# A top-1 expert layer that sorts its tokens through DRAM and runs each tile of 128 rows through one expert

## The reference

```python
router_logits = x @ Wr.T
expert_idx = jnp.argmax(jax.nn.softmax(router_logits, axis=-1), axis=-1)
inter = jnp.zeros((x.shape[0], W1.shape[2]), dtype=x.dtype)          # [2048, 512]
for e in range(E):
    mask = (expert_idx == e)[:, None].astype(x.dtype)
    inter = inter + mask * jax.nn.gelu(x @ W1[e] + b1[e], approximate=False)
y = inter @ Wo + bo + x
out = (y - mu) * jax.lax.rsqrt(var + LN_EPS) * gamma + beta          # mean and variance of y
...
x = x + 0.5 * _L0_ffn_ref(_layernorm(x, axis=-1), ...)
```

## Time and profile before

| | us |
|---|---|
| median of three runs | 1225.09 (1223.17 to 1226.32) |
| the profiled execution, its own time | 1229.85 |
| its span in the trace | 1227.9 |
| TensorE (matmul) busy | 1100.5 (90%) |
| VectorE busy | 1005.6 (82%) |
| ScalarE busy | 665.1 (54%) |
| GpSimd busy | 65.8 (5%) |
| first matmul of the second expert layer starts at | 604.06 |
| first result of the ternary layer behind it (L982) starts at | 749.19 |

### The profile page before, as it was taken

How to read it: one execution, slowest core, us unless ns; L and a number is a source line. 1 busy time by engine, 2 the same in 40 slices (tenths; PEclk the granted TensorE clock), 3 DMA queues, 4 the chain that set the end, 5 groups by cost and what they waited for, 6 DMA issues and landing times.

```text
span 1227.9 us, 33848 instructions
## 1 busy us (share of the span) xinstructions
PE 1100.5 (90%) x14565; PEld 487.3 (40%) x14565; DVE 1005.6 (82%) x2343; ACT 665.1 (54%) x861; POOL 65.8 (5%) x62
## 2 busy tenths in 40 slices
PE   1998977999999999998699979589999999999978
PEld 1455542333333333333355547333333333333336
DVE  8977569999999998885447557789999999987754
ACT  0322222556777777777332214145667777787753
POOL 5111001000000000000101000100000000000000
PEclk9999988999999999999699999799999999999998
DMA  5100044000000000000000000620000000000001
GB/s 157 36 1 1 1 119 121 5 3 3 2 2 2 3 2 2 3 3 3 1 1 1 1 1 1 181 63 3 2 2 2 3 2 2 2 2 3 3 2 35
DMA packets 23554, 24.05 MB, mean 20 GB/s; under 512 B 3134, under 2 KB 21220, under 8 KB 23404
## 3 DMA queue, kind: packets, MB, share of 16 engines
q1 hardware_dynamic: 22252, 18.73, 5.3%
q0 software_dynamic: 1152, 3.15, 0.9%
HBM read 13.20 MB, written 8.39 MB: 18 GB/s over the span
## 4 chain that ended last, share of the span: by engine, by line
PE 52%; DVE 37%; issue 4%; ACT 4%; DMA 1%; SPq 0%; DVEq 0%; ACTq 0%
DVE part_max L1349 26%; PE psum L1209 11%; PE psum L1231 10%; PE psum L443 10%; PE psum L1183 6%; ACT hidden L1312 3%; PE psum L467 3%; PE psum L1196 2%; PE psum L899 2%; PE psum L914 1%; DVE xn L168 1%; PE psum L1258 1%; PE psum L1237 1%; DVE norm_v L151 1%; PE psum L428 1%
## 5 line engine op out<-in xcount | busy, mean ns | idle before, releaser
L1349 DVE TENSOR_REDUCE part_max<-psum 128x1 f32<-128x512 f32 (+3 forms) x1120 | 676.6, 666 | 59.9 <-PE psum L1237 40.4
L1312 ACT ACTIVATE hidden<-psum 128x1024 f32<-128x1024 f32 (+3 forms) x640 | 538.7, 895 | 231.0 <-PE psum L1196 127.3
L1231 PE MATMUL psum<-k_slots,q_slots 128*32 128x512 f16 (+3 forms) x5120 | 391.0, 355 | 32.9 <-DVE part_max L1349 13.5
L1209 PE MATMUL psum<-hidden,v_aug 128*9 128x512 f32 (+3 forms) x2560 | 291.8, 532 | 0.4 <-ACT hidden L1312 0.4
L1231 PEld LDWEIGHTS psum<-k_slots,q_slots 128*32 128x32 f16 x5120 | 123.5, 95 | 289.2 <-DVE part_max L1349 194.1
L443 PE MATMUL psum<-parts,w_parts 128*128 128x512 f16 x768 | 179.7, 385 | 1.9 <-DVE parts L839 1.9
L1183 PE MATMUL psum<-q_slots,k_slots 32*128 32x512 f16 (+3 forms) x1280 | 146.1, 354 | 18.0 <-ACT hidden L1312 14.0
L443 PEld LDWEIGHTS psum<-parts,w_parts 128*128 128x128 f16 x768 | 73.7, 99 | 82.5 <-issue 5.9
L1183 PEld LDWEIGHTS psum<-q_slots,k_slots 32*128 32x128 f16 x1280 | 43.0, 91 | 146.0 <-ACT hidden L1312 85.1
L587 ACT CAST parts<-psum 128x512 f16<-128x512 f32 x64 | 37.2, 588 | 107.3 <-PE psum L428 107.3
L1237 PE MATMUL psum<-ident_bf,later_keys 128*32 128x128 bf16 (+2 forms) x1408 | 91.8, 251 | 0.0
(11 more groups left out here) (168 smaller groups left out, 721.6 us busy)
## 6 DMA issues: line engine op xcount, KB each, us to landing
q_slots<-q_rows SPq DMA_DIRECT2D x8, 512.0 KB, 3.7
k_slots<-k_rows POOLq DMA_DIRECT2D x24, 128.0 KB, 4.1
q_rows<-parts SPq DMA_DIRECT2D x18, 128.0 KB, 2.9
k_rows<-parts SPq DMA_DIRECT2D x18, 128.0 KB, 2.7
q_slots<-in_L_ffn_W_dram SPq DMA_DIRECT2D x2, 1024.0 KB, 6.8
k_slots<-k_rows SPq DMA_DIRECT2D x8, 128.0 KB, 3.9
q_slots<-nm_parts SPq DMA_DIRECT2D x64, 4.0 KB
out_dram<-x_res SPq DMA_DIRECT2D x4, 256.0 KB, 2.3
```

Source lines behind the costliest of these rows:

```text
L1209: last = pe.matmul(psum[VW * h:VW * h + DH + 1, O_BANK, off:CH], v_aug[:, j, G * g + h, :], probs[:, (2 * n + h // 2) % NP, h % 2, off:CH] ...
L1231: last = pe.matmul(psum[rows32(m), bank, a * w:(a + 1) * w], q_slots[:, g, qb * P + m * SLOT:qb * P + (m + 1) * SLOT], k_slots[:, G * g + ...
L1312: act.activation(probs[:, tile % NP, :, off:CH], psum[:, bank:bank + 2, off:CH], ACT.Exp, scale=scale).then_inc(exp_done, 1)
L1349: dve.tensor_reduce(part_max[:, step_no[s] % 2, h0:h0 + heads, i, kc], psum[:, bank, 0:heads * w].rearrange("p (a k) -> p a k", a=heads), ...
```

## The change

The third layer is now `sorted_expert_layer` (after: L914 to L1287). The first layer is still `expert_layer`.

*Routing.* All four chunks are turned, given logits and `onehot`, and in addition each token's row in a DRAM table is counted out with small matmuls (`ranks`): expert e's region starts at row 2048 e, and a token's row there is how many earlier tokens chose e. GpSimd writes the blocks of `xn` there with 16 indirect DMAs of 128 rows. `tile_table` counts how many tiles of 128 rows each expert needs, gives each of 24 tiles an expert and a start, and puts them into `tile_i`. 24 tiles always suffice, and all 24 are always run.

*Experts.* SyncE waits for all scatters and loads the 24 tiles into `x_sorted`, each with a start read from `tile_i` into a register. Six groups of four tiles then take the place of four chunks of eight masked experts. The expert's weights are picked by a register, so the masks, their copies and products are gone; a group is 4 bias matmuls of 512 columns and 48 of 128 columns.

*Way back.* A finished group is scaled by gamma on GpSimd and stored by SyncE to `sorted_dram`. When all six are stored, GpSimd fetches each token's row by 16 indirect DMAs that add to `x_res`; the next layer normalises a chunk once its four have landed. Of the next layer's chunks one is normalised in this layer (`next_given` = 1) and three in the ternary layer.

*First layer.* 17 short GpSimd instructions set constants, and SyncE writes zeros over the DRAM table, 8 MB in two DMAs. A few semaphores are merged.

```diff
+            @blk.tensor
...
+                def ranks(n):
+                    pe.wait_ge(onehot_ready, n + 1)
...
+                    for i in range(BPC):
+                        out_i = psum[:, RANK_BANK, i * E:(i + 1) * E]
+                        pe.matmul(out_i, ones_bf[:, :], region_rows[:, :], start=True, stop=False)
+                        if n:
+                            pe.matmul(out_i, ones_bf[:, :], before[:, :], start=False, stop=False)
+                        for j in range(i):
+                            pe.matmul(out_i, ones_bf[:, :], onehot[:, n * BPC + j, 0, :], start=False, stop=False)
+                        last = pe.matmul(out_i, earlier[:, :], onehot[:, n * BPC + i, 0, :], start=False, stop=True)
+                    last.then_inc(ranked, 1)
...
+                def experts(n):
...
+                    chosen = [pe.value_load(tile_i[0:1, 0, n * BPC + i:n * BPC + i + 1], min_val=0, max_val=E - 1)
+                              for i in range(BPC)]
+                    pe.wait_ge(lo_ready, n + 1)
+                    for t in range(HT):
+                        if n >= 1:
+                            pe.wait_ge(gelu_done, HT * (n - 1) + t + 1)
+                        pe.matmul(psum[:, t, :], b1_parts[:, t * P:(t + 1) * P],
...
+                        for i in range(BPC):
+                            for wp, xp in ((0, 0), (0, 1), (1, 0)):
+                                weights = w1_parts[:, bass.ds(chosen[i], 1), wp, t * P:(t + 1) * P]
+                                last = pe.matmul(psum[:, t, i * P:(i + 1) * P], weights.rearrange("p a i -> p (a i)"),
+                                                 x_parts[:, n % 2, xp, i * P:(i + 1) * P], start=False,
+                                                 stop=(i, wp) == (BPC - 1, 1))
+                        last.then_inc(experts_done, 1)
...
+                pe.wait_ge(*released)
+                transposes(0)
+                logits(0)
+                for n in range(NCH):
+                    if n + 1 < NCH:
+                        transposes(n + 1)
+                    ranks(n)
+                    if n + 1 < NCH:
+                        logits(n + 1)
+                tile_table()
+                sorted_transposes(0)
+                for n in range(TGROUPS):
+                    experts(n)
+                    if n + 1 < TGROUPS:
+                        sorted_transposes(n + 1)
+                    if n >= 1:
+                        down(n - 1)
+                down(TGROUPS - 1)
...
+            @blk.gpsimd
...
+                for n in range(NCH):
...
+                    pool.wait_ge(placed, n + 1)
+                    for i in range(BPC):
+                        b = n * BPC + i
+                        pool.indirect_dma_start(out=region_dram, out_offset=bass.IndirectOffsetOnAxis(place[:, b:b + 1], 0),
+                                                in_=xn[:, lo + i, :], in_offset=None).then_inc(scattered, 16)
...
+                for n in range(TGROUPS):
+                    pool.wait_ge(group_moved[n], STORED)
+                for c in next_norms.order:
+                    for i in range(BPC):
+                        b = order.index(c) * BPC + i
+                        pool.indirect_dma_start(out=x_res[:, c * BPC + i, :], out_offset=None, in_=sorted_dram,
+                                                in_offset=bass.IndirectOffsetOnAxis(back[:, b:b + 1], 0),
+                                                compute_op=ALU.add).then_inc(arrived[c], 16)
...
+            @blk.vector
...
+                for n in range(NCH):
+                    choose(n)
+                    if given <= n + 1 < NCH:
+                        norms.make(dve, own, s1, order[n + 1])
+                    take_places(n)
+                tile_table()
+                ways_back()
+                low_part(0)
+                for n in range(TGROUPS):
+                    if n + 1 < TGROUPS:
+                        low_part(n + 1)
+                    finish(n)
+                for c in next_norms.order[:next_given]:
+                    next_norms.make(dve, own, s1, c)
...
+            @blk.sync
+            def _(sp):
+                sp.wait_ge(table_ready, 1)
+                sp.wait_ge(scattered, 16 * NB)
+                for k in range(TILES):
+                    start = sp.value_load(tile_i[0:1, 1, k:k + 1], min_val=0, max_val=E * T - P)
+                    sp.dma_start(x_sorted[:, k, :], region_dram[bass.ds(start, P), :]).then_inc(group_moved[k // BPC], 16)
...
-        released = expert_layer(False, orders[2], 2, norms[2], norms[3], released)
-        released = ternary_layer(False, orders[3], 3, norms[3], norms[4], released, projections[4])
+        released = sorted_expert_layer(orders[2], 2, norms[2], norms[3], 1, released)
+        released = ternary_layer(False, orders[3], 1, norms[3], norms[4], released, projections[4])
```

More of the change, by code:

```diff
@@ L31 @@
 NPART = 3
+TILES = 24
+TGROUPS = TILES // BPC
+assert TILES >= NB + E - 1
 TERMS = 3
@@ L179, in __init__ @@
                 self.ready, self.order = sem(name), order
+                self.arrived = None
             def wait(self, engine, chunk):
@@ L184, in make @@
             def make(self, dve, own, scratch, chunk):
+                if self.arrived:
+                    dve.wait_ge(self.arrived[chunk], 16 * BPC)
                 norm_stats(dve, own, scratch, x_res, chunk * BPC, BPC)
@@ L376, in _ @@
                     sp.wait_ge(b1_split_ready, 1)
+                    sp.wait_ge(sorting_set, 2)
                     for r in range(NPART):
@@ L386, in _ @@
                                  k_slots[0:H * MAX_PARTS, 0, :]).then_inc(rest_rows_stored, 16)
-                    sp.wait_ge(rest_rows_stored, 16 * 3)
+                    zeros = k_slots[:, 2:2 + H // 2, :].rearrange("p h t -> p (h t)").bitcast(F32)
+                    for half in range(2):
+                        rows = slice(half * E * T // 2, (half + 1) * E * T // 2)
+                        sp.dma_start(region_dram[rows, :].rearrange("(p r) d -> p (r d)", p=P),
+                                     zeros).then_inc(rest_rows_stored, 16)
+                    sp.wait_ge(rest_rows_stored, 16 * 5)
                     sp.wait_ge(b1_moved, 16 * NPART)
@@ L405, in logits @@
                     if first and n == 0:
-                        pe.wait_ge(wr_ready, 1)
+                        pe.wait_ge(weights_on_dve, 2)
                     for i in range(BPC):
@@ L452, in biases @@
                     for t in range(HT):
-                        pe.matmul(psum[:, t, :], b1_parts[:, t * P:(t + 1) * P], onehot_t[:, n % 2, :],
+                        pe.matmul(psum[:, t, :], b1_parts[0:NPART * E, t * P:(t + 1) * P], onehot_t[:, n % 2, :],
                                   start=False, stop=True).then_inc(experts_done, 1)
@@ L1449, in macaron_layers @@
         orders = (UP, UP, BETWEEN, TURNING, TURNING, DOWN)
-        norms = [Norms(f"xn_ready{i}", order) for i, order in enumerate((UP, UP, BETWEEN, BETWEEN, TURNING, DOWN))]
+        norms = [Norms(f"xn_ready{i}", order) for i, order in enumerate((UP, UP, BETWEEN, TURNING, TURNING, DOWN))]
         projections = {1: Projection(w_qkv0, False, norms[1], orders[1]), 4: Projection(w_qkv1, True, norms[4], orders[4])}
```

323 lines of the change are left out of this document (299 added, 24 removed).

## The result

The changed kernel takes 1270.82 us in the median of four runs (1265.44 to 1273.12) against 1225.70 (1223.17 to 1228.45) of the kernel before on the same chip: a ratio of 1.036 (95% interval 1.032 to 1.040). It is 45 us slower. The forecast was 1286 us in a range of 1258 to 1320. The profiled execution took 1273.08 us.

What follows compares the result with a forecast made beforehand. TensorE was taken to set the pace before; afterwards a serial chain: 51.3+114.5+20.7+19.5 = 206.0 us against 145.1, +60.9, so 1290.8 us profiled and 1286 as a median, range 1258 to 1320.

Steps and rivals of the forecast that it cites:

- A: Routing, from the layer's first matmul until group 0's tiles have landed: 51.3 us.
- B: The six expert groups, from first tile's turning to the last finish: 114.5 us.
- C: Way back: scaling, store, four gathers and landing, normalising, turn, high and low part, all open: 20.7 us.
- D: Ternary layer up to its first result, with three more chunks normalised in the open: 19.5 us.
- the serial turn: Groups 2 to 5: experts, turning, down, finish, low part without overlap, W + 10.4 us; W 7.5 to 10.5, 1277 to 1295, 55%.
- rival 3: Six groups: the group is cheap, W 5.4 to 7, 12 to 22 us less, 1264 to 1274; 17%.
- W: TensorE's expert matmuls of one group: taken as 9 us, bounds 5.4 and 12.4.
- Rival 2: Six groups: slow on TensorE, W = 12.4 gives 1306, a clock staying at 1.2 GHz 1323; 22%.
- The registers' 2 us: Share of each group's expert time on TensorE allowed for register instructions: 2 us.
- Rival 4: Six turns: TensorE's work alone paces, 128-column matmul 0.054, W 3.5, turn 7.7, groups 54, time 1226, not slower; 3%.
- The four landings on the chain: DMA landings of scatter, tile load, store and fetch: 12.8 us from profile rows; 9 by the skill's fit, giving 1282.
- The first layer: Zeroing the DRAM table done near 106 us, before SyncE is next wanted at 154.92: costs nothing.

Runs made afterwards that it cites:

- Experiment 1: Changed kernel with VectorE making the low part of group n+2 ahead of finish(n), not behind it: 1242.91 us, median of four.
- experiment 6: Changed kernel with low parts ahead of finish and tile k fixed to expert k mod 8, no register loads: 1232.36 us, one run.
- experiment 3: Changed kernel with tile k fixed in code to expert k mod 8, no expert registers, output not the reference's: 1271.25 us, one run.
- experiment 7: Experiment 5 plus expert registers loaded inside down(n) and late chunks normalised one choice earlier: 1221.53 us, median of ten, ratio 0.9973 to the kernel before.
- experiment 2: Changed kernel with GpSimd's four beta additions moved behind the last scatter: 1263.36 us, one run.
- experiment 4: Changed kernel with the 16 final indirect fetches writing x_res without adding, output not the reference's: 1262.30 us, one run.
- experiment 5: Changed kernel with low parts ahead, beta additions late, and the ternary layer's fb_half additions on VectorE instead of GpSimd: 1236.41 us, one run.
- experiment 8: Experiment 7 with plain fetches into xn and VectorE adding each chunk to x_res before normalising: 1224.83 us, median of ten, ratio 0.9990 to the kernel before.

## Why the prediction was right, and where its numbers were not

Forecast and measured costs are +60.9 and +44.5 us for the stage. The difference of 16.4 is A -2.8, B -18.8, C +0.3 and D +5.0. That the total is no further off is in part luck: D's error hides 5 us of B's, and A and C are each a sum of errors that cancel.

**The mechanism: right.** The forecast was the serial turn, and everything said of its order is in the trace: `finish` then low part, over 6 us of waiting for L1230, on groups 2 to 5, with the granted clock below 1. Experiment 1 shows it by taking it away. The time is that of rival 3 (1264 to 1274), the same serial turn with a W of 5.4 to 7, which had been given 17%; the forecast's own W of 7.5 to 10.5, with 55%, did not come. The signs read the same way: the wait is there, but turns are 15.5 to 16.7 us apart for 19 to 20, not far above the 15 at which the forecast called itself wrong, L1040 is busy 5.0 us a group for 9, and the last `finish` ends at 748.83 for 770. Rival 2, a clock that stays low, is half there: groups start low and all recover within the group, and down (3.74 us) runs at the full level.

**The mis-sized term: W.** "I take 7 for a group half at the low clock plus 2 for the registers: W = 9." Measured from a group's first bias matmul to the start of what follows it W is 6.39, 4.29, 5.11, 5.85, 6.24 and 6.44, mean 5.7: 19.7 us less over six, which is more than piece B's whole error. B without W is 61.3, forecast 60.5. Two terms failed. The registers' 2 us were the right price in the wrong place: 1.8 a turn where TensorE paces (experiments 1 and 6), nothing behind a wait (3). And 0.095 us for a 128-column pair was read from the length of a group of four (0.38). Such a length contains the whole of one matmul, from start to end: that is 0.219 us, yet 12 take 0.83, which is 0.219 + 11 x 0.0555. The price in a running sequence is 0.0555, a quarter of the 0.216 of 512 columns. Rival 4 had that figure (0.054), and its turn of 7.7 us is the 7.56 of experiments 6 and 7, with the order mended. Its point, "It decides from turns of 7.6 us down", does not hold by the turn alone: in experiment 6 piece B is 59.1 where rival 4 had 54, and the kernel took 1232. Experiment 7 came out 0.3% below the kernel before with what pieces A and D gave besides. With 0.0555 the bounds of W would have been 3.5 and, four feature tiles at 1.2 GHz, about 6.8; all six groups lie between.

**Piece A: 48.5 for 51.3, two errors of opposite sign.** `ranks` was priced at 1.8 and 2.3 us of small matmuls. Its matmuls of 8 columns follow each other every 0.026 us, so a chunk's are over in 0.5 to 0.7. That error, some 6 us over four chunks, was largely offset by the 4.6 us that GpSimd's additions cost, holding VectorE and the last scatters (experiment 2), which the prediction had not counted. Scatters come every 1.27 us for the 1.2 taken, and the 24 tile loads are issued every 1.1, as taken.

**Piece C: 21.0 for 20.7, by luck.** Four fetches took 7.2 us for 4.8, and VectorE starts at 762.32, 1.8 us after the fourth was issued, where 4.1 had been taken for the landing: +2.4 and -2.3. The four landings on the chain, 12.8 us in the forecast, measured 2.2 (scatter), 1.7 (tile load), 2.3 (store) and 3.3 (fetch) from the start of their issue, 9.5 together. The estimated 9 us that the prediction worked out beside the rows was nearer, though two of the four are issued by SyncE, and the page of the Trainium skill that it took the fit from, DMA: Bandwidth & Descriptors, section Anatomy of one DMA, gives it for DMAs that GpSimd issues.

**Piece D: 24.5 for 19.5.** "1.3 on GpSimd" was one addition at its own price. It missed that two additions queue behind 16 fetches and then hold VectorE, 3.5 us (experiments 4 and 5).

**The first layer: right.** SyncE's first attention DMA starts at 154.20 us, where it was 154.92; the zeros delay nothing.

## What to carry to other kernels

When a change takes work off the engine that paced a loop, look at what paces the loop next; here it was the order of the instructions on the other engines. Write out, for one turn, which instruction of each engine stands ahead of the one that is waited for, and move the producer for the next turn ahead of the long consumer of this one. Here that one move of a 0.7 us instruction was worth 28 us. Price short instructions by their start-to-start spacing in a long row, never by the length of a group of a few; and let GpSimd's elementwise work run only where VectorE is not on the chain.

## What had not been expected of the hardware

- An elementwise addition of 128x512 on GpSimd (1.27 us) can hold even a VectorE operation of four elements a partition until it ends: 1.97 us for 0.16. A VectorE operation with one of its two inputs in PSUM was not held (0.69 us as elsewhere, experiment 2).
- An indirect DMA of 128 rows that adds is issued every 1.86 us, one that doesn't every 1.26.
- TensorE's sequencer takes 0.30 us to load a register from SBUF, 0.15 for what follows it, and 0.046 for each of 192 address computations. Behind a wait for VectorE none of it showed (experiment 3); at the head of a group in a loop that TensorE paced it was 1.8 us a turn (1 against 6); with the loads spread between the matmuls of `down` the turn was 7.56 us, as without registers (7 and 6).
- A result of TensorE reached VectorE 1.6 to 2.5 us late in the routing of experiments 5 to 8, and within 0.11 us in the changed kernel. Why is open.
